# Feed-forward rows of 13 tiles: turned by a transposing DMA in place of TensorE

## What is computed

```python
def fp4_quant_dequant(x):          # blocks of 16 along the last dimension
    scale = jnp.maximum(jnp.max(jnp.abs(xb), axis=-1, keepdims=True) / 6.0, jnp.float32(1e-12))
    idx = jnp.searchsorted(_MID, jnp.abs(xb / scale))
    return (_GRID[idx] * jnp.sign(xn) * scale).reshape(shape)

x = x + xattn(layernorm(x), ctx, ctx, ...)
h = silu(fp4_linear(layernorm(x), w_gate)) * fp4_linear(layernorm(x), w_up)   # 256 -> 704
x = x + fp4_linear(h, w_down)                                                 # 704 -> 256
```

## Time and profile before

| | us |
|---|---|
| median of 3 runs (lowest to highest) | 424.98 (424.27 to 427.12) |
| profiled execution, its own time | 426.62 |
| span of the profiled execution, first to last instruction | 424.8 |
| busy in the span: PE / PEld | 342.5 / 257.3 |
| busy in the span: DVE / ACT / POOL | 319.3 / 262.0 / 254.2 |
| mean granted TensorE clock, share of full | 0.964 |

### The profile page before, as it was taken

How to read it: one execution, slowest core, us unless ns; L and a number is a source line. 1 busy time by engine, 2 the same in 40 slices (tenths; PEclk the granted TensorE clock), 3 DMA queues, 4 the chain that set the end, 5 groups by cost and what they waited for, 6 DMA issues and landing times.

```text
span 424.8 us, 9531 instructions
## 1 busy us (share of the span) xinstructions
PE 342.5 (81%) x3595; PEld 257.3 (61%) x3595; DVE 319.3 (75%) x634; ACT 262.0 (62%) x635; POOL 254.2 (60%) x248
## 2 busy tenths in 40 slices
PE   1877567799898878988879777479778999999985
PEld 1554355577666666766667565356555777677764
DVE  2978445657876688767878985367999999999692
ACT  3655677777797887877878688532451535543331
POOL 6361233746768786678777757524783777686610
PEclk9989689999999999999999999689898999999999
DMA  7971335646768787797888678701100000000001
GB/s 220 322 287 31 64 62 80 128 88 104 129 133 152 139 128 135 132 141 138 130 154 138 132 104 159 142 2 30 35 0 15 12 26 12 26 14 13 27 25 39
DMA packets 125375, 40.86 MB, mean 96 GB/s; under 512 B 117452, under 2 KB 123280, under 8 KB 125329
## 3 DMA queue, kind: packets, MB, share of 16 engines
q1 hardware_dynamic: 125329, 40.25, 47.5%
HBM read 8.78 MB, written 2.10 MB: 26 GB/s over the span
## 4 chain that ended last, share of the span: by engine, by line
DVE 44%; ACT 20%; PE 19%; issue 10%; POOL 5%; DMA 1%; SPq 0%; ACTq 0%; DVEq 0%
ACT arena L831 10%; DVE negmax L1069 8%; PE ps L483 5%; PE ps L485 4%; PE ps L484 4%; DVE arena L1085 4%; DVE arena L1146 4%; DVE arena L1148 3%; DVE arena L1100 3%; DVE arena L1267 3%; DVE arena L1233 2%; POOL arena L1338 2%; ACT arena L841 2%; POOL arena L1343 2%; DVE arena L1104 2%
## 5 line engine op out<-in xcount | busy, mean ns | idle before, releaser
L1338 POOL TENSOR_TENSOR arena<-arena 128x640 f16<-128x640 f32 x64 | 89.6, 1400 | 87.2 <-ACT arena L841 86.8
L831 ACT ACTIVATE arena<-ps,negmax 128x154 f32<-128x154 f32 x256 | 78.8, 392 | 50.0 <-DVE negmax L1069 50.0
L562 PE MATMUL ps<-v_h,pT 128*128 128x132 f16 (+1 forms) x640 | 51.9, 211 | 13.2 <-DVE q_odd L1061 7.2
L1343 POOL TENSOR_TENSOR arena<-arena 128x256 f16<-128x256 f32 x64 | 50.5, 791 | 8.7 <-ACT arena L848 8.7
L562 PEld LDWEIGHTS ps<-v_h,pT 128*128 128x128 f16 x640 | 37.9, 98 | 22.2 <-issue 20.9
L1069 DVE TENSOR_REDUCE negmax<-ps 128x4 f32<-128x616 f32 x64 | 50.6, 791 | 0.3 <-PE ps L617 0.2
L483 PE MATMUL ps<-arena 128*128 128x256 f16 (+1 forms) x144 | 42.0, 292 | 8.4 <-DVE arena L974 6.0
L841 ACT ACTIVATE arena<-arena 128x640 f16<-128x640 f32 x64 | 48.5, 757 | 0.1
L483 PE MATMUL ps<-arena,xnT_even 128*128 128x352 f16 x128 | 41.0, 320 | 4.2 <-DVE xnT_even L1156 4.2
L484 PE MATMUL ps<-arena 128*128 128x256 f16 (+1 forms) x144 | 41.8, 290 | 0.0
L485 PE MATMUL ps<-arena 128*128 128x256 f16 (+1 forms) x144 | 41.8, 290 | 0.0
(11 more groups left out here) (155 smaller groups left out, 951.8 us busy)
## 6 DMA issues: line engine op xcount, KB each, us to landing
out_dram<-arena SPq DMA_DIRECT2D x16, 128.0 KB, 1.7
pT<-arena SPq DMA_TRANSPOSE x70, 4.0
xs<-in_x_dram SPq DMA_DIRECT2D x2, 512.0 KB, 7.2
arena<-in_L_xattn_w_out_dram SPq DMA_DIRECT2D x1, 1024.0 KB, 12.0
xs<-in_x_dram SPq DMA_DIRECT2D x2, 384.0 KB, 6.6
wffn<-in_L_ffn_w_down_dram SPq DMA_DIRECT2D x1, 704.0 KB, 9.6
wffn<-in_L_ffn_w_gate_dram SPq DMA_DIRECT2D x1, 640.0 KB, 7.6
wffn<-in_L_ffn_w_up_dram SPq DMA_DIRECT2D x1, 640.0 KB, 8.5
```

The lines of the kernel that those rows point to most:

```text
L562: last = pe.matmul(o[:, h0 * HB:h1 * HB], pT[:, n % RING_P, part * CHUNKS + c], v[:, b, j, at[0]:at[-1] + 1].rearrange("p m k -> p (m k)") ...
L831: last = act.activation(prob[:, j, k * LP:k * LP + L], ps[:, 2 * (j % 2) + k % 2, (k // 2) * L:(k // 2 + 1) * L], ACT.Exp, bias=negmax[:, ...
L1338: pool.tensor_tensor(part_of(j, 1), prob[:, j], part_of(j, 0), ALU.subtract).then_inc(p_low, 1)
L1343: pool.tensor_tensor(hid_part(n, 1), hidden_f[:, n % 2], hid_part(n, 0), ALU.subtract).then_inc(hid_low, 1)
```

## The change

The gated rows of tiles 0 to 12 are no longer turned by TensorE. ScalarE copies `hq` to float16 in SBUF (`high_h`), GpSimd subtracts it from `hq` and writes the rest as float16 (`low_h`), and a transposing DMA issued by SyncE turns both parts at once, from `hsplit` to `hT`. `down` waits for the DMA. Tiles 13, 14 and 15 are turned by TensorE as before, with `high_ht` and `low_ht`. The factor -16 that the two reads of PSUM had applied is put into the block scales of the quantisation.

```diff
+BY_PE = 3
...
-        hT_h, hT_l = (take(FP_).bitcast(F16).rearrange("p (s n) -> p s n", s=2) for _ in range(2))
+        hT = take(2 * FP_).bitcast(F16).rearrange("p (s a n) -> p s a n", s=2, a=2)
+        hsplit = raw["q"][:, 0:2 * FP_].bitcast(F16).rearrange("p (s a n) -> p s a n", s=2, a=2)
...
+        TURNED_BY_PE = 2 * STEPS - BY_PE
...  (SyncE)
+            def turn_h(t):
+                i, s = step_of(t)
+                sp.wait_ge(h_low, t + 1)
+                if t == 0:
+                    for j in range(QUADS):
+                        sp.wait_ge(turned[j], 16 * len(range(j, SLOTS + HID_LAG, QUADS)))
+                wait(sp, down_mm, t - 1)
+                sp.dma_start_transpose(hT[:, s].rearrange("p a (c n) -> p (a c) n", n=P),
+                                       hsplit[:, s].rearrange("p a n -> p (a n)")).then_inc(h_turned[s], 16)
...
+            for t in range(2 * STEPS):
+                if t < TURNED_BY_PE: turn_h(t)
+                if t >= DOWN_LAG - 2: store(t - DOWN_LAG + 2)
+            for t in range(2 * STEPS - DOWN_LAG + 2, 2 * STEPS):
+                store(t)
...  (TensorE)
             def down(i, s):
-                pe.wait_ge(ht_low, t + 1)
+                if t < TURNED_BY_PE:
+                    pe.wait_ge(h_turned[s], 16 * (t // 2 + 1))
+                else:
+                    pe.wait_ge(ht_low, t - TURNED_BY_PE + 1)
...
-                    if exists(turned[0]): turn_h(*turned)
...  (ScalarE)
+            def high_h(t):
+                act.wait_ge(hq_done, t + 1)
+                wait(act, h_turned[t % 2], 16 * (t // 2))
+                if t == 0: act.wait_ge(pad2_zero, 2)
+                act.activation(hsplit[:, t % 2, 0, 0:F], hq[:, t % 2, 0:F], ACT.Copy).then_inc(h_high, 1)
...
             def ffn(i):
                 for s in range(B):
+                    t = 2 * i + s
+                    if 0 <= t - 2 < TURNED_BY_PE: high_h(t - 2)
                     silu_gate(i, s)
...
-                    if exists(turned[0]): h_high(*turned)
...  (VectorE)
-                    elif exists(shift(i, s, -TURN_LAG)[0]):
-                        h_low(*shift(i, s, -TURN_LAG))
-                    if last_tile(i, s): quantise_last(i, s)
+                        low_ht(TURNED_BY_PE)
+                        quantise_last(i, s)
...  (GpSimd)
+            def low_h(t):
+                pool.wait_ge(h_high, t + 1)
+                pool.tensor_tensor(hsplit[:, t % 2, 1, 0:F], hq[:, t % 2, 0:F], hsplit[:, t % 2, 0, 0:F], ALU.subtract).then_inc(h_low, 1)
...
                     if s == 1 and exists(i + 2): value_x(i + 2)
+                    if 0 <= 2 * i + s - 2 < TURNED_BY_PE: low_h(2 * i + s - 2)
                     if not last_tile(i, s): value_h(i, s)
...
                     if exists(shift(i, s, -1)[0]): round_h(*shift(i, s, -1))
```

More of the change, by code:

```diff
@@ L259, in xattn_ffn_kernel @@
         ht_mm, ht_high, ht_low = sem("ht_mm"), sem("ht_high"), sem("ht_low")
+        h_high, h_low = sem("h_high"), sem("h_low")
+        h_turned = [sem("h_turned0"), sem("h_turned1")]
         down_mm, y_ready = sem("down_mm"), sem("y_ready")
@@ L466, in _, with store @@
                 turn(n)
[L468 to L474, removed]
+            def turn_h(t):
[7 more added lines that the diff above has]
+                                       hsplit[:, s].rearrange("p a n -> p (a n)")).then_inc(h_turned[s], 16)
+            def store(t):
+                i, s = step_of(t)
+                sp.wait_ge(y_ready, t + 1)
+                sp.dma_start(out[batch(i), rows_of(i, s), :], y[:, s, :]).then_inc(stored[s], 16)
+            for t in range(2 * STEPS):
[3 more added lines that the diff above has]
+                store(t)
             for s in range(B):
@@ L683, in gate_up, with turn_h @@
                 last.then_inc(gu_mm, 1)
-            def turn_h(i, s):
-                t = 2 * i + s
-                if last_tile(i, s):
+            def turn_h(t):
+                s = t % 2
+                if t == 2 * STEPS - 1:
                     pe.wait_ge(hq_last, LAST_STEPS)
@@ L690, in turn_h @@
                     pe.wait_ge(hq_done, t + 1)
-                if t == 0: pe.wait_ge(pad2_zero, 2)
-                if ht_bank(i, s) == HT_BANK:
-                    wait(pe, ht_low, t - 2 if last_tile(i, s) else t)
+                if t == TURNED_BY_PE:
+                    pe.wait_ge(pad2_zero, 2)
                 else:
@@ L696, in turn_h @@
                 for c in range(FC):
-                    last = pe.transpose(ps[:, ht_bank(i, s) + c // 4, (c % 4) * P:(c % 4 + 1) * P],
-                                        hq[:, s, c * P:(c + 1) * P], ident[:, :])
+                    last = pe.transpose(ht_banks(t)[:, c * P:(c + 1) * P], hq[:, s, c * P:(c + 1) * P], ident[:, :])
                 last.then_inc(ht_mm, 1)
@@ L707, in down @@
                 for c in range(FC):
-                    last = three(ps[:, D_BANK, 0:D], hT_h[:, s, c * P:(c + 1) * P], hT_l[:, s, c * P:(c + 1) * P],
+                    last = three(ps[:, D_BANK, 0:D], hT[:, s, 0, c * P:(c + 1) * P], hT[:, s, 1, c * P:(c + 1) * P],
                                  wdT[:, c, 0:D], wdT[:, c, D:2 * D], False, c == FC - 1)
@@ L713, in ffn @@
                 for s in range(B):
-                    turned, summed = shift(i, s, -TURN_LAG), shift(i, s, -DOWN_LAG)
+                    summed = shift(i, s, -DOWN_LAG)
                     gate_up(i, s)
@@ L731, in _ @@
             last = 2 * STEPS - 1
-            turn_h(*step_of(last - 2))
+            turn_h(last - 2)
             down(*step_of(last - 3))
-            turn_h(*step_of(last - 1))
+            turn_h(last - 1)
             down(*step_of(last - 2))
-            turn_h(*step_of(last))
+            turn_h(last)
             down(*step_of(last - 1))
@@ L946, in _ @@
             last = 2 * STEPS - 1
-            h_high(*step_of(last - 2))
+            high_ht(last - 2)
             y_copy(*step_of(last - 3))
-            act.wait_ge(down_mm, last - 2)
-            h_high(*step_of(last - 1))
+            high_ht(last - 1)
             y_copy(*step_of(last - 2))
-            act.wait_ge(down_mm, last - 1)
-            h_high(*step_of(last))
+            high_ht(last)
             y_copy(*step_of(last - 1))
@@ L1239, in scales_h @@
                 dve.wait_ge(hid_ready, t + 1)
-                block_scales(hid[:, s], [blk_h[:, s, r] for r in range(3)], hscaled, t)
+                block_scales(hid[:, s], [blk_h[:, s, r] for r in range(3)], hscaled, t, -HS)
             def grid_h(i, s):
@@ L1256, in quantise_last @@
                 dve.wait_ge(hscaled, 3 * t + 3)
-                then(dve.tensor_tensor(blocks(v), blocks(hid[:, s]), spread(blk_h[:, s, 2]), ALU.mult), 1)
+                then(dve.scalar_tensor_tensor(blocks(v), blocks(hid[:, s]), -HS, spread(blk_h[:, s, 2]), ALU.mult, ALU.mult), 1)
                 then(dve.tensor_scalar(e.bitcast(I32), v.bitcast(I32), 0x7F800000, None, ALU.bitwise_and), 2)
@@ L1343, in low_hid, with value @@
                 pool.tensor_tensor(hid_part(n, 1), hidden_f[:, n % 2], hid_part(n, 0), ALU.subtract).then_inc(hid_low, 1)
[L1345 removed]
+            def value(v, src, r, scaled, lowered, valued, t, by=0):
                 pool.wait_ge(scaled, 3 * t + 3)
[L1348 removed]
+                pool.tensor_tensor(r[3], r[2], below[:, by:by + 1].to_broadcast([P, r[2].shape[1]]), ALU.mult).then_inc(lowered, 1)
                 pool.wait_ge(lowered, t + 1)
@@ L1387, in value_h @@
                 t = 2 * i + s
-                value(h_tmp[s][0], hid[:, s], [blk_h[:, s, r] for r in range(4)], hscaled, hlowered, hvalued, t)
+                value(h_tmp[s][0], hid[:, s], [blk_h[:, s, r] for r in range(4)], hscaled, hlowered, hvalued, t, 1)
+            def low_h(t):
+                pool.wait_ge(h_high, t + 1)
+                pool.tensor_tensor(hsplit[:, t % 2, 1, 0:F], hq[:, t % 2, 0:F], hsplit[:, t % 2, 0, 0:F], ALU.subtract).then_inc(h_low, 1)
             def round_h(i, s):
                 t = 2 * i + s
-                wait(pool, ht_mm, t - 1)
+                if t >= TURNED_BY_PE + 2: pool.wait_ge(ht_mm, t - 1 - TURNED_BY_PE)
                 pool.wait_ge(hgrid, t + 1)
@@ L1405, in ffn @@
                             pool.wait_ge(turned[j], 32 * STEPS)
-                        pool.memset(hq[:, :, F:FP_], 0.0).then_inc(pad2_zero, 1)
+                        pool.memset(hq[:, :, F:FP_], 0.0)
+                        pool.memset(hsplit.rearrange("p s a n -> p (s a) n")[:, :, F:FP_], 0.0).then_inc(pad2_zero, 1)
                     if exists(shift(i, s, -1)[0]): round_h(*shift(i, s, -1))
```

38 lines of the change are left out of this document (17 added, 21 removed).

## The result

The changed kernel takes 443.38 us in the median (442.90 to 444.91, 4 runs) and the kernel before, beside it, 425.70 (424.27 to 427.12, 4 runs): a ratio of 1.0422, 95% interval 1.0375 to 1.0468. It is slower by 17.7 us; the prediction was 443.0 and slower. The profiled execution took 443.32 us with a span of 441.5.

A forecast was written before the change was run, and what follows sets the result against it. VectorE bounds the feed-forward stage before; after, a loop through ScalarE's queue takes 17.77 us per two tiles in place of 15.10. Summed over the tiles, 17.9 us added to 424.98 gives 443 us, range 432 to 456.

The forecast's parts named there:

- The loop through ScalarE's queue: Feed-forward stage: Silu queues behind the copy waiting for GpSimd's rounding; two tiles take 17.77 us in place of 15.10.
- The pieces: The loop's length per tile, scales to rounding to Silu to scales: even 8.86 us, odd 8.91.
- Scales to rounding: From the end of VectorE's scales to the end of GpSimd's rounding: 4.25 us even, 4.70 odd.
- Rounding to Silu: From the rounding's end through ScalarE's new copy to Silu's start: 0.71 us, bounds 0.65 and 0.81.
- Silu to the end of the scales: From Silu's start on ScalarE to the end of VectorE's scales: 3.90 us even, 3.50 odd.
- The sum: Silu starts added up from tile 2 to the end: span 442.7 us, 17.9 longer, so 443 in the median.
- What was taken at nothing: Costed at zero: GpSimd's subtraction in the steady loop, the DMA, the transposes off TensorE and L915 off ScalarE.
- The microsecond at the entry: At the stage's start, `low_h(0)` behind the last attention subtraction meets the scales: 1.0 us, bounds 0 and 1.39.
- Subtraction finds no cover: Rival: GpSimd's `low_h` runs into L1102 and `value_h`, 3 to 15 us more, 451 in its middle; chance 0.13.
- TensorE's clock: Rival: after waits gate and up run at 1.2 GHz, taking 7.2 us; 4 to 10 us more, 450; chance 0.07.
- Not slower: Rival: the loop doesn't outgrow 7.55 us a tile, only the entry's 2 to 3 us stay, 428; chance 0.07.
- Faster: Rival: VectorE's relief comes through as the copy's wait is over in time; 12.4 us less, 413; chance 0.05.

The follow-up runs named there:

- the last order: Changed kernel with ScalarE's copy moved behind `magnitude_h` and GpSimd's subtraction moved behind the rounding, all work done: 429.20 us, ratio 1.0089.

## Why the prediction was right

**The loop through ScalarE's queue.** Right, and shown from both sides: with the copy out of Silu's way, or with its rounding a tile further back, the pair falls from 17.81 to between 15.2 and 15.5 us in the mean, and a longer copy lengthens every loop by the 0.68 us that it adds ahead of Silu.

**The pieces.** Scales to rounding: 348.20 to 352.45 = 4.25 in an even iteration (said: 4.25) and 4.71 in an odd one (4.70). Rounding to Silu: 0.73 (0.71). Silu to the end of the scales: 348.20-344.28 = 3.92 (3.90) and 3.47 (3.50). They could hold because `grid_h` still runs beside `value_h`, as both start when the scales end (GpSimd's value and rounding behind the scales of tile 6 take 1.98 and 1.38 us, before and after), so rows of before measured the very meetings that the new loop has. In one piece there was luck: no row had the new copy, 0.71 was picked between 0.65 and 0.81, and a tenth more would have been 1.3 us over 13 loops.

**The sum.** Silu of tiles 2, 3, 4, 5, 6, 12 and 14 was put at 303.3, 314.4, 323.3, 336.9, 345.8, 399.1 and 416.0, and starts at 301.75, 312.90, 321.81, 335.37, 344.28, 397.71 and 414.62, 1.4 to 1.6 us earlier throughout. That offset is there before the first new wait, as the rounding of tile 0 ended 1.6 earlier in this execution; from Silu(2) on no step is off by more than 0.15. Tile 15's `hidden` came 6.63 after Silu(14) (6.6), and the rest took 441.5-421.25 = 20.25 (20.1).

**What was taken at nothing.** The subtraction, rightly, though its row was off: it takes 1.52 us with a float16 result, where 1.39 was taken from float32 rows. Its cover was 1.5 us in the steady loop, not under one, because `scales_x`, which `value_x` waits for, is done while VectorE waits. The microsecond at the entry (L1121 at 1.23) is there, and the run without the subtraction shows it to be the subtraction's. The DMA too: its 13 transposes land after 3.7 us in the median, and no `down` waits. The transposes taken from TensorE and L915 from ScalarE are in none of the loop's pieces; no run tests them by themselves.

**The rivals.** *Subtraction finds no cover*: refuted by the run without it (its own bounds, 3 and 15 us, have their middle at 452, not 451). Its mechanism is real, though, and it becomes the bound as soon as the loop is open. *TensorE's clock*: the clock fell as said, but in part of the tiles only, and the slowed gate and up of tile 7 take 352.05-346.78 = 5.27 us in place of 3.59, not 7.2, since only their first half runs at the low level; they end at 352.2, before the copy starts at 352.49. *Not slower* needed the piece from the scales to the rounding at 3.2 us, and it stayed at 4.25 and 4.71. *Faster*: the wait would have had to be over before gate and up end, and 65.2 us of it are measured. Its price of 12.4 us was too high as well: with the wait and the subtraction both gone, the stage is 6.3 us shorter than before.

## To carry to other kernels

Before placing a step that waits for another engine at the head of an in-order queue, follow the queue from there until it comes back to what the step waits for, and add up the pieces: if they come to more than the present rhythm of a tile, that sum is the new rhythm, whatever the step itself costs. Taking work off such a loop's side branch changed nothing here (443.05 us without the subtraction, 443.38 with it), and the same work binds once the loop is open (8.7 us), so the value of removing a step has to be asked in the order in which the kernel would be left. Where the moved work lands on an engine whose instructions lengthen those of the relieved one, as GpSimd's and VectorE's do here, price it there too.

## What the runs showed of the hardware

- GpSimd's subtraction of 704 elements into float16 takes 1.51 to 1.53 us in the changed kernel, and 1.96 to 2.13 in two of the other orders, where it starts while VectorE's grid instruction runs; a float32 result of the same size took 1.39.
- The load of one engine shows in the durations of the other: VectorE's grid instruction of 704 elements takes 0.83 us in the changed kernel, 1.75 with the copy last and 1.81 with the lag of one tile more, where it starts while the subtraction runs, and 1.66 in the last order, beside GpSimd's value.
- The transposing DMA from SBUF to SBUF is quick enough at the distance of the change, and not at one tile less: TensorE then waits 10.6 us for it over eight tiles (between 300 and 410 us). The changed kernel's DMA view (operation, count, median us to landing):

```profile
arena<-arena SPq DMA_TRANSPOSE x13, 3.7
```

- A granted clock of 0.50 in a window cost nothing in the steady loop (443.73 us without it, 443.38 with it), and 1.5 us at the one tile whose Silu no copy held up.
